# A mixture-of-experts kernel on one core: the first search candidates in one operation, one-hot rows tile by tile, w2's last quarters behind the first tokens, the last block in halves

## The chip, the core and the metric

The kernel runs on one core of a Trainium2 chip. The metric is the device time of one execution in microseconds, and the number that counts is the median of several runs. The engines of a core work beside each other and meet at semaphores: TensorE (PE) multiplies matrices, VectorE (DVE), ScalarE (ACT) and GpSimd (POOL) work on rows, SyncE (SP) issues plain transfers, and GpSimd issues the gathers and scatters by index.

## What is computed

```python
x = x + tanh(g_xattn) * wkv(time_decay, time_first, k=layernorm(x), v=ctx)   # 8 x 256 tokens, 512 channels
f = layernorm(x).reshape(2048, 512)
logits = f @ Wg + bg                       # 4 experts
top_vals, top_idx = top_k(logits, 2)
probs = softmax(logits kept at the top 2, -inf elsewhere)
out = zeros_like(f)
for i in range(4):
    score = where(expert i is in the top 2, probs[:, i], -inf)
    sel_p, sel_idx = top_k(score, 512)     # the expert takes its 512 best tokens
    p = where(isfinite(sel_p), sel_p, 0)
    h = gelu(f[sel_idx] @ W1[i])           # 512 x 2048
    out = out.at[sel_idx].add((h @ W2[i]) * p)
x = x + tanh(g_ffn) * out
```

## The kernel before, in words

**Stages.** From 0 to about 95 us the attention part runs, channel tile by channel tile (a scan on VectorE), and writes the new x to the result and its normalised rows to a table in HBM (`xn2_table`). Then comes the router, then for each expert a list of 512 tokens. The rows of the list are gathered from the table into `tok` (4 tiles of 128 tokens), transposed by TensorE, and split into a high and a low f16 half (`tok_hi` by ScalarE, `tok_lo` by VectorE). The weights are split in the same way, after a scale is taken from their magnitudes (`w1_hi`, `w1_lo`, `w2_hi`, `w2_lo`). Each product is thus three f16 products. The hidden rows are made in 16 blocks of 128, four PSUM banks at a time; for expert 0 the first four blocks are made in `first_group` (L742), token half by token half, the other twelve in `first_up` (L779), for experts 1 to 3 all in `up_product` (L801). Behind them `down_block` (L816) makes the output of 128 tokens at a time: 48 products of 512 columns (16 hidden blocks, three products each), scaled by VectorE (`take_y`, L1732) and added to the result by a scatter of GpSimd (L1213).

**The list of expert 0.** The smallest probability still taken is found digit by digit: six rounds of 5 bits (`ROUNDS0`, `DIGIT0`). Each of 128 partitions holds one candidate of 32 (`LANES0`). A round is, on VectorE: count how many probabilities reach the candidate (L1531), spread the count over the lanes (`spot`, L1540), a small step of other work (`between(r)`), then, when TensorE has added the counts over the partitions (L657), count the lanes that reach 512 (`reached`, L1543), take the digit from it (L1546), and make the next candidate from digit and `nxt` (L1549, L1552). `base` holds the digits found (L1533, L1535), `nxt` is base with the next round's lane (L1538); both stand ahead of `spot`. Then come the prefix sums, `slot_b` and `slot_a` (a token's place within a tile of the list, and the tile), `in_a`, `put` (L1646), and the one-hot rows `hot`: 16 token tiles of 128 columns, in two operations of 8 tiles (L1653). TensorE multiplies `hot` by `put`, 8 products per operation (L690), and the result is the list (`idx`, L1662).

**Order around it.** All orders are written by hand. ScalarE takes, in this order: the w1 halves, the magnitudes of w2's second quarter, a copy for the other experts' search, the copies `tok_hi` of tokens 0 and 1 (L1078), the magnitudes of w2's third quarter (L1024), the copies of tokens 2 and 3, the magnitudes of the fourth. VectorE: the lows of both token halves (L1739), the first quarter of w1_lo (L1684), `wtop` from w2's magnitudes (L1677), a step of the other experts' search, `wall` (L1462; it needs a transpose of `wtop`, which TensorE does behind the products of the second half), the scale, the second quarter of w1_lo; for this last one `first_up` waits. TensorE: two rounds for the other experts with four products between them that only keep it busy (`keep_warm`, L718), the transposes of tokens 0 and 1 (L734), the high products of the first half, the transposes of tokens 2 and 3, the low products, then the same of the second half.

**Transfers.** SyncE issues w2 of expert 0 in four quarters of 1 MB (`first_w2`, L535), the last three in a row behind the stores of x1 and of the table. GpSimd gathers once with indices that are all zero into the fourth tile of `tok` (L1228) before the list is there, and issues the fourth real gather behind its landing; then it issues the four gathers of `gather(0)` (L1204). The small constant matrices `less16`, `group16` and `tri16` are made on VectorE, within the search.

## Time and profile before

| | us |
|---|---|
| median of 3 runs | 478.41 (478.31 to 478.71) |
| the profiled execution | 478.91 |
| its span | 477.1 |
| TensorE busy | 414.5 (87%) |
| ScalarE busy | 310.1 (65%) |
| VectorE busy | 293.1 (61%) |
| GpSimd busy | 107.2 (22%) |

The profile is of one execution; times in it count from the start of its span. A row of a timeline says when an instruction started, how long it took, on which engine and line, and in brackets how long the engine had stood idle before it and what released it. Idle time of an engine matters only where others wait for it.

### The profile page before, as it was taken

To read this page: it belongs to the slowest core of one execution; us is meant where nothing else is said; L and a number is where in the kernel's file an instruction comes from. 1 tells how busy PE (TensorE), PEld (TensorE's weight loads), DVE (VectorE), ACT (ScalarE), POOL (GpSimd) and SP (SyncE) were. 2 spreads that over 40 slices of the span, in tenths; PEclk is the share of its full clock that TensorE was granted. 3 is DMA by queue.
4 is the path that set the end of the run, shared out by engine and by line. 5 is a ranking of instruction groups with operands and counts; after the bars stand their busy time and mean duration, and the time that the engine had idled before them with its cause. 6 is when DMAs were issued, how large, how long until landed. Compare 5 with 4: busy or idle time off the path is not lost.

```text
span 477.1 us, 7133 instructions
## 1 busy us (share of the span) xinstructions
PE 414.5 (87%) x2039; PEld 201.4 (42%) x2039; DVE 293.1 (61%) x600; ACT 310.1 (65%) x477; POOL 107.2 (22%) x122
## 2 busy tenths in 40 slices
PE   2586877812799999999999999999999999999991
PEld 2342433401564444454444444444444444444440
DVE  7999999988499976564675156357514635560000
ACT  6578888998569873936778790577879147770000
POOL 0777746601300002521001311100041110001111
PEclk9999998965699999999999999999999999999996
DMA  7984120399400829439001925600093310001211
GB/s 263 341 354 177 44 77 13 141 344 357 149 1 1 326 91 311 97 61 350 0 0 44 374 63 174 228 0 1 3 371 88 42 26 0 0 0 9 36 22 22
DMA packets 23126, 59.64 MB, mean 125 GB/s; under 512 B 1280, under 2 KB 1408, under 8 KB 21056
## 3 DMA queue, kind: packets, MB, share of 16 engines
q1 hardware_dynamic: 19008, 50.17, 28.4%
q0 software_dynamic: 3664, 8.65, 9.0%
q10 hardware_dynamic: 432, 0.54, 0.3%
q8 instruction: 11, 0.18, 0.1%
q14 instruction: 11, 0.09, 0.1%
HBM read 46.78 MB, written 12.58 MB: 124 GB/s over the span
## 4 chain that ended last, share of the span: by engine, by line
PE 73%; DVE 18%; issue 3%; ACT 2%; DMA 2%; POOL 0%; DVEq 0%; POOLq 0%
PE ps L816 35%; PE ps L801 26%; DVE arena L1275 7%; PE ps L779 7%; PE ps L742 2%; DVE arena L1294 2%; DVE arena L1305 2%; DVE bn L1260 1%; PE ps L712 1%; DMA arena<-xn_table,idx 1%; DVE arena L1531 1%; DMA small<-in_scalars 1%; DVE arena L1282 1%; DVE arena L1290 1%; PE ps L734 1%
## 5 line engine op out<-in xcount | busy, mean ns | idle before, releaser
L816 PE MATMUL ps<-arena 128*128 128x512 f16 x768 | 167.7, 379 | 0.0
L801 PE MATMUL ps<-arena,early 128*128 128x512 f16 x576 | 124.8, 379 | 0.0
L816 PEld LDWEIGHTS ps<-arena 128*128 128x128 f16 x768 | 74.7, 98 | 88.0
L801 PEld LDWEIGHTS ps<-arena,early 128*128 x576 | 56.4, 98 | 68.0
L1042 ACT ACTIVATE arena<-ps,up 128x512 f32<-128x512 f32 x64 | 43.8, 684 | 58.5 <-PE ps L801 40.0
L1704 DVE SCALAR_TENSOR_TENSOR arena<-arena,h_down 128x512 f32 x48 | 36.1, 751 | 58.9 <-ACT arena L1045 58.9
L1213 POOL DMA_INDIRECT result<-arena,idx x16 | 27.6, 1723 | 191.4 <-DVE arena L1732 137.8
L1045 ACT ACTIVATE arena<-arena,h_down 128x512 f32 x64 | 46.2, 721 | 8.7 <-ACT arena L1042 0.2
L1684 DVE SCALAR_TENSOR_TENSOR early<-w_raw,down,early 128x2048 f16<-128x2048 f32 x16 | 37.1, 2346 | 18.9 <-ACT early L1003 18.8
L1732 DVE TENSOR_SCALAR arena<-ps,yscale 128x512 f32<-128x512 f32 x16 | 12.0, 748 | 58.6 <-PE ps L816 49.1
L1048 ACT ACTIVATE arena<-rows,down x64 | 45.2, 706 | 0.0
L1003 ACT ACTIVATE early<-w_raw,down 128x2048 f16<-128x2048 f32 x16 | 30.7, 1990 | 14.6 <-DVE down L1479 14.6
L1204 POOL DMA_INDIRECT arena<-xn_table,idx x16 | 16.6, 1036 | 97.1 <-DVE plist L1667 93.2
L570 PE MATMUL ps<-cst,early 128*128 128x128 f32 x64 | 13.8, 329 | 27.0 <-DVE arena L1290 11.9
L1275 DVE TENSOR_TENSOR_SCAN arena<-arena,ps 128x1024 f32<-128x1024 f32 (+1 forms) x20 | 37.0, 1852 | 0.0
L1707 DVE SCALAR_TENSOR_TENSOR arena<-rows,down,arena x48 | 35.8, 746 | 0.0
L1024 ACT ACTIVATE arena<-rows 128x2048 bf16<-128x2048 f32 x16 | 30.4, 1900 | 1.7 <-DMA rows<-in_L_ffn_W 1.7
L779 PE MATMUL ps<-arena,early 128*128 128x512 f16 x144 | 31.4, 379 | 0.0
L1011 ACT ACTIVATE arena<-w_raw 128x2048 bf16<-128x2048 f32 x12 | 22.8, 1897 | 2.9 <-DVE arena L1714 1.8
L1143 POOL TENSOR_TENSOR arena<-arena 128x512 f32<-128x512 f32 (+1 forms) x19 | 20.4, 1074 | 17.9 <-ACT arena L938 17.5
L570 PEld LDWEIGHTS ps<-cst,early 128*128 128x128 f32 x64 | 8.1, 160 | 34.8 <-DVE arena L1290 17.3
L779 PEld LDWEIGHTS ps<-arena,early 128*128 128x128 f16 x144 | 13.7, 97 | 16.8 <-DVE early L1684 0.4
(226 smaller groups left out, 457.4 us busy)
## 6 DMA issues: line engine op xcount, KB each, us to landing
w_raw<-in_L_ffn_W SPq DMA_DIRECT2D x4, 4096.0 KB, 13.7
rows<-in_L_ffn_W SPq DMA_DIRECT2D x3, 4096.0 KB, 17.9
rows<-in_L_ffn_W SPq DMA_DIRECT2D x4, 1024.0 KB, 9.2
result<-rows SPq DMA_DIRECT2D x3, 1024.0 KB, 6.8
early<-in_ctx SPq DMA_DIRECT2D x2, 1024.0 KB, 6.6
rows<-in_x SPq DMA_DIRECT2D x2, 1024.0 KB, 11.8
xn_table<-arena SPq DMA_DIRECT2D x4, 512.0 KB, 5.2
xn_table<-arena SPq DMA_DIRECT2D x2, 1024.0 KB, 4.6
```

Of the source, the lines that this page charges most:

```text
L779: last = nc.tensor.matmul(ps[:, PH[q], :], w[:, k, b * P:(b + 1) * P], t[:, k, :], start=n == 0, stop=n == 3 * CT - 1)
L801: last = nc.tensor.matmul(ps[:, PH[q], :], w[:, k, at], t[:, k, :], start=n == 0, stop=n == 3 * CT - 1)
L816: last = nc.tensor.matmul(ps[:, PY[s % 2], :], h[:, t, s * P:(s + 1) * P], w[:, t, :], start=t == 0 and n == 0, stop=t == HT - 1 and n == 2)
L1003: nc.scalar.activation(w1_hi[:, k, :], w1_raw[:, k, :], ACT.Copy, scale=down[:, 0:1]).then_inc(c_w1hi, 1)
L1024: nc.scalar.activation(spent[:, k % 2, :], some, ACT.Abs, scale=1.0 / (HT * D // CT), accum_out=wmax[:, 1, k:k + 1]).then_inc(c_w2sum, 1)
L1042: nc.scalar.activation(h_f[:, q, :], ps[:, PH[q], :], ACT.Gelu, scale=up[:, 0:1]).then_inc(c_gelu, 1)
L1045: nc.scalar.activation(h_hi[:, bass.ds(at, 1), :].rearrange("p a d -> p (a d)"), h_f[:, q, :], ACT.Copy, scale=h_down[:, 0:1]).then_inc(c_ ...
L1048: nc.scalar.activation(w2_hi[:, bass.ds(at, 1), :].rearrange("p a d -> p (a d)"), w2_raw[:, bass.ds(at, 1), :].rearrange("p a d -> p (a d) ...
L1275: nc.vector.tensor_tensor_scan(state[:, u % 2, 1:size + 1], decay[:, u % CT, 0:size], pair(u, 0, size), 0.0, ALU.mult, ALU.add).then_inc(s ...
L1684: nc.vector.scalar_tensor_tensor(w1_lo[:, :, some], w1_raw[:, :, some], down[:, 0:1], w1_hi[:, :, some], ALU.mult, ALU.subtract).then_inc( ...
L1704: nc.vector.scalar_tensor_tensor(row(h_lo), h_f[:, q, :], h_down[:, 0:1], row(h_hi), ALU.mult, ALU.subtract).then_inc(c_hlo, 1)
L1707: nc.vector.scalar_tensor_tensor(row(w2_lo), row(w2_raw), down[:, 1:2], row(w2_hi), ALU.mult, ALU.subtract).then_inc(c_w2lo, 1)
```

## The change

It does the following.

- **Search.** For the first three rounds (`EXACT0` = 3) the next candidate comes in one operation from the number of lanes reached (`took`), as took x step + a prepared sum; the constant table has three more columns for it (`C_NEXT0`). The sums (`sum_next`, `sum_base`) are made by `add_steps`, behind `spot`. `base` and `nxt` stand behind `spot` in all rounds. The rounds from the fourth on keep digit and candidate apart.
- **One-hot rows.** `first_slots` makes expert 0's `hot` in 16 operations of 128 columns, from an f16 row of 0 to 127 (`iota16`) and `slot_f`, a float copy of `slot_b`; TensorE waits tile by tile.
- **Small matrices.** `less16`, `group16`, `tri16` and `iota16` are made on GpSimd, ahead of the lists.
- **Transfers.** The gather with zero indices is gone. SyncE waits for the landing of tokens 0 and 1 before it issues the third and fourth quarter of w2.
- **keep_warm.** Four more products that only keep TensorE busy stand ahead of the first tokens.
- **Last block.** The last 128 tokens of expert 3 are computed in two column halves of 256, in two PSUM banks (`last_halves`), each scaled, and scattered to a view of the result in half rows, with the indices `idx_half`.

```diff
-C_ALL = C_LANE0 + ROUNDS0
+C_NEXT0 = C_LANE0 + ROUNDS0
+EXACT0 = 3
+C_ALL = C_NEXT0 + EXACT0
...
+def ones0(r):
+
+    return sum(1 << shift0(i) for i in range(r + 1))
...
-    t[:, C_LANE0:] = np.concatenate([lane << shift0(r) for r in range(ROUNDS0)], 1).astype(np.int32).view(np.float32)
+    for r in range(EXACT0):
+        t[:, C_NEXT0 + r] = (lane[:, 0] << shift0(r + 1)) - ones0(r)
+    t[:, C_LANE0:C_NEXT0] = np.concatenate([lane << shift0(r) for r in range(ROUNDS0)], 1).astype(np.int32).view(np.float32)
...
             first_w2(1, (2,))
+            for k in range(SPT):
+                sp.wait_ge(c_tok[k], 16)
             first_w2(2, (3,))
             first_w2(3, (4,))
...
             for t in range(TT):
-                if t % (TT // 2) == 0:
-                    pe.wait_ge(b_hot, t // (TT // 2) + 1)
+                pe.wait_ge(b_hot, t + 1)
                 last = nc.tensor.matmul(ps[:, PI, 0:ST * 4], hot[:, t, :], put[:, 0, t, :], start=t == 0, stop=t == TT - 1)
             last.then_inc(b_hotused, 1)
...
                 keep_warm(WARM)
                 others_round(1)
+                keep_warm(WARM)
                 pe.wait_ge(b_taken, 2)
...
+            def last_halves():
+
+                for n in range(2):
+                    cols = slice(n * D // 2, (n + 1) * D // 2)
+                    pe.wait_ge(c_yout, START + (E - 1) * ST + (ST - 2))
+                    for t in range(HT):
+                        for i, (h, w) in enumerate(((h_hi, w2_hi), (h_hi, w2_lo), (h_lo, w2_hi))):
+                            last = nc.tensor.matmul(ps[:, LAST[n], 0:D // 2], h[:, t, (ST - 1) * P:ST * P], w[:, t, cols],
+                                                    start=t == 0 and i == 0, stop=t == HT - 1 and i == 2)
+                    last.then_inc(c_y, 1)
...
-            for s in range(ST):
+            for s in range(ST - 1):
                 down_block(E - 1, s)
+            last_halves()
...
+            pool.wait_ge(s_cst, 16)
+            nc.gpsimd.tensor_copy(iota16[:, :], cst[:, C_IOTA:C_IOTA + P]).then_inc(s_lists, 1)
+            nc.gpsimd.tensor_scalar(less16[:, :], cst[:, C_TRI:C_TRI + P], -1.0, None, ALU.add).then_inc(s_lists, 1)
+            nc.gpsimd.tensor_copy(group16[:, :], cst[:, C_GRP:C_GRP + P]).then_inc(s_lists, 1)
+            nc.gpsimd.tensor_copy(tri16[:, :], cst[:, C_TRI:C_TRI + P]).then_inc(s_lists, 1)
...
-            nc.gpsimd.memset(none[:, :], 0).then_inc(c_zero, 1)
-            pool.wait_ge(c_zero, 1)
-            nc.gpsimd.indirect_dma_start(tok[:, ST - 1, :], None, xn2_table, bass.IndirectOffsetOnAxis(ap=none[:, 0:1], axis=0),
-                                         bounds_check=N - 1, compute_op=ALU.bypass).then_inc(c_none, 16)
             gather(0)
...
-            scatter(E - 1, range(ST))
-            added(E - 1)
+            scatter(E - 1, range(ST - 1))
+            pool.wait_ge(c_yscs, START + 2 * E + 2)
+            for n in range(2):
+                cols = slice(n * D // 2, (n + 1) * D // 2)
+                pool.wait_ge(c_yout, START + (E - 1) * ST + ST + n)
+                hold(pool, "pool")
+                nc.gpsimd.indirect_dma_start(out_halves, bass.IndirectOffsetOnAxis(ap=idx_half[:, n:n + 1], axis=0),
+                                             y_c[:, (ST - 1) % 2, cols], None,
+                                             bounds_check=2 * N - 1, compute_op=ALU.add).then_inc(c_last[n], 16)
...
+            def add_steps(r):
+
+                size = float(1 << shift0(r - 1))
+                if r > 1:
+                    dve.wait_ge(b_sums, made[r - 2])
+                if r < EXACT0:
+                    for k in range(r, EXACT0):
+                        plus = cst[:, C_NEXT0 + k:C_NEXT0 + k + 1] if r == 1 else sum_next[:, k - 1:k]
+                        nc.vector.tensor_scalar(sum_next[:, k - 1:k], took[:, r - 1:r], size, plus, ALU.mult, ALU.add).then_inc(b_sums, 1)
+                    plus = -float(ones0(EXACT0 - 1)) if r == 1 else sum_base[:, r - 2:r - 1]
+                    nc.vector.tensor_scalar(sum_base[:, r - 1:r], took[:, r - 1:r], size, plus, ALU.mult, ALU.add).then_inc(b_sums, 1)
+                else:
+                    nc.vector.tensor_scalar(base[:, 0:1], took[:, r - 1:r], size, sum_base[:, r - 2:r - 1],
+                                            ALU.mult, ALU.add).then_inc(b_base, 1)
 
...
-                if r == 1:
-                    nc.vector.tensor_copy(base[:, 0:1], digit[:, 0:1]).then_inc(b_base, 1)
-                if r > 1:
-                    nc.vector.tensor_tensor(base[:, 0:1], base[:, 0:1], digit[:, 0:1], ALU.bitwise_or).then_inc(b_base, 1)
-                if 0 < r < ROUNDS0 - 1:
-                    dve.wait_ge(b_base, r)
-                    nc.vector.tensor_tensor(nxt[:, 0:1], base[:, 0:1], lane0(r + 1), ALU.bitwise_or).then_inc(b_next, 1)
                 dve.wait_ge(b_cnt, r + 1)
                 nc.vector.tensor_scalar(spot[:, :], cst[:, C_ONE0:C_ONE0 + LANES0], cnt[:, 0:1], None, ALU.mult).then_inc(b_spot, 1)
+                if 0 < r <= EXACT0:
+                    add_steps(r)
+                if r > EXACT0:
+                    nc.vector.tensor_tensor(base[:, 0:1], base[:, 0:1], digit[:, 0:1], ALU.bitwise_or).then_inc(b_base, 1)
+                if EXACT0 <= r < ROUNDS0 - 1:
+                    dve.wait_ge(b_base, r - EXACT0 + 1)
+                    nc.vector.tensor_tensor(nxt[:, 0:1], base[:, 0:1], lane0(r + 1), ALU.bitwise_or).then_inc(b_next, 1)
                 between(r)
                 dve.wait_ge(b_lane_n, r + 1)
                 nc.vector.tensor_scalar(reached[:, :], ps[:, PC, 0:LANES0], float(CAP), None, ALU.is_ge, ALU.add,
-                                        accum_out=steps_up[:, 0:1]).then_inc(b_reached, 1)
+                                        accum_out=took[:, r:r + 1]).then_inc(b_reached, 1)
                 dve.wait_ge(b_reached, r + 1)
-                nc.vector.tensor_scalar(digit[:, 0:1], steps_up[:, 0:1], -1.0, float(1 << shift0(r)), ALU.add, ALU.mult).then_inc(b_digit, 1)
-                dve.wait_ge(b_digit, r + 1)
-                if r == 0:
-                    nc.vector.tensor_tensor(cand[:, 0:1], digit[:, 0:1], lane0(1), ALU.bitwise_or).then_inc(b_cand, 1)
-                elif r < ROUNDS0 - 1:
-                    dve.wait_ge(b_next, r)
+                if r < EXACT0:
+                    if r > 0:
+                        dve.wait_ge(b_sums, summed[r - 1])
+                    plus = cst[:, C_NEXT0:C_NEXT0 + 1] if r == 0 else sum_next[:, r - 1:r]
+                    nc.vector.tensor_scalar(cand[:, 0:1], took[:, r:r + 1], float(1 << shift0(r)), plus,
+                                            ALU.mult, ALU.add).then_inc(b_cand, 1)
+                else:
+                    nc.vector.tensor_scalar(digit[:, 0:1], took[:, r:r + 1], -1.0, float(1 << shift0(r)), ALU.add, ALU.mult).then_inc(b_digit, 1)
+                    dve.wait_ge(b_digit, r - EXACT0 + 1)
+                if EXACT0 <= r < ROUNDS0 - 1:
+                    dve.wait_ge(b_next, r - EXACT0 + 1)
                     nc.vector.tensor_tensor(cand[:, 0:1], digit[:, 0:1], nxt[:, 0:1], ALU.bitwise_or).then_inc(b_cand, 1)
-            dve.wait_ge(b_base, ROUNDS0 - 1)
+            dve.wait_ge(b_base, ROUNDS0 - EXACT0)
...
-            step(nc.vector.tensor_scalar(slot_a[:, 0, :], posi[:, 0, :], 7, None, ALU.logical_shift_right), 2)
+            nc.vector.tensor_scalar(slot_a[:, 0, :], posi[:, 0, :], 7, None, ALU.logical_shift_right).then_inc(b_dve, 1)
+            steps[0] += 2
+            dve.wait_ge(b_dve, steps[0] - 1)
+            step(nc.vector.tensor_copy(slot_f[:, :], slot_b[:, 0, :]))
...
+            def first_slots():
+
+                nc.vector.tensor_tensor(put[:, 0, :, :].rearrange("p t (a c) -> p t a c", a=ST),
+                                        in_a[:, 0].unsqueeze(3).to_broadcast([P, TT, ST, 4]),
+                                        vals[:, 0].unsqueeze(2).to_broadcast([P, TT, ST, 4]), ALU.mult)
+                dve.wait_ge(s_lists, 1)
+                for t in range(TT):
+                    nc.vector.tensor_scalar(hot[:, t, :], iota16[:, :], slot_f[:, t:t + 1], None, ALU.is_equal).then_inc(b_hot, 1)
...
+                dve.wait_ge(b_taken, 2 * E)
+                nc.vector.tensor_scalar(idx_half[:, n:n + 1], idx[:, E - 1, ST - 1:ST], 1, n,
+                                        ALU.logical_shift_left, ALU.bitwise_or).then_inc(c_yscs, 1)
+            for s in range(ST - 1):
                 take_y(E - 1, s)
...
+            dve.wait_ge(c_add[1], 16 * ((E - 1) * (ST // 2) + 1))
+            for n in range(2):
+                cols = slice(n * D // 2, (n + 1) * D // 2)
+                dve.wait_ge(c_y, START + (E - 1) * ST + ST + n)
+                nc.vector.tensor_scalar(y_c[:, (ST - 1) % 2, cols], ps[:, LAST[n], 0:D // 2], yscale[:, ST - 1:ST], None,
+                                        ALU.mult).then_inc(c_yout, 1)
```

On VectorE, the third round of expert 0's search (its start is the count with `cand`) in the kernel before, and then in the changed one:

```order
L1531 TENSOR_SCALAR arena,cnt<-ps,cand 128x512
L1535 TENSOR_TENSOR base<-base,digit 128x1
L1538 TENSOR_TENSOR nxt<-base,cst 128x1
L1540 TENSOR_SCALAR spot<-cst,cnt 128x32
L1462 TENSOR_REDUCE wall<-ps 128x1
L1543 TENSOR_SCALAR reached,steps_up<-ps 128x32
L1546 TENSOR_SCALAR digit<-steps_up 128x1
L1552 TENSOR_TENSOR cand<-digit,nxt 128x1
```

Two operations stand ahead of `spot`, and two between reached and the next count. Changed:

```order
L1586 TENSOR_SCALAR arena,cnt<-ps,cand 128x512
L1588 TENSOR_SCALAR spot<-cst,cnt 128x32
L1563 TENSOR_SCALAR sum_next<-took,sum_next 128x1
L1565 TENSOR_SCALAR sum_base<-took,sum_base 128x1
L1502 TENSOR_REDUCE wall<-ps 128x1
L1598 TENSOR_SCALAR reached,took<-ps 128x32
L1605 TENSOR_SCALAR cand<-took,sum_next 128x1
```

`spot` follows its count directly, two sums stand behind it, and one operation instead of two lies between reached and the next count.

On VectorE, from the places to the list of expert 0, before and then changed:

```order
L1569 TENSOR_SCALAR slot_b<-posi 128x16
L1570 TENSOR_SCALAR slot_a<-posi 128x16
L1571 TENSOR_TENSOR in_a<-slot_a,cst 128x64
L1646 TENSOR_TENSOR put<-in_a,vals 128x256
L1653 TENSOR_TENSOR arena<-cst,slot_b 128x1024 x2
L1662 CAST idx<-ps 128x4
```

The whole of `hot` is two operations. Changed:

```order
L1629 TENSOR_SCALAR slot_b<-posi 128x16
L1630 TENSOR_SCALAR slot_a<-posi 128x16
L1633 CAST slot_f<-slot_b 128x16
L1634 TENSOR_TENSOR in_a<-slot_a,cst 128x64
L1709 TENSOR_TENSOR put<-in_a,vals 128x256
L1714 TENSOR_SCALAR arena<-iota,slot_f 128x128 x16
L1734 CAST idx<-ps 128x4
```

Sixteen operations stand for two, and the `slot_f` cast is new.

On SyncE, the transfers around w2's quarters (rows<-in_L_ffn_W) in the changed kernel, with the semaphores that each waits for:

```order
L542 DMA xn_table<-arena 128x2x512 [waits last_xn2_ready,xn2_ready]
L549 DMA rows<-in_L_ffn_W 128x4x512 [waits x1_stored_2]
L549 DMA rows<-in_L_ffn_W 128x4x512 [waits x1_stored_3,tokens_landed_1,tokens_landed_0]
L549 DMA rows<-in_L_ffn_W 128x4x512 [waits x1_stored_4]
L564 UNCONDITIONAL_BRANCH
```

Before, the third and fourth quarter waited for the stores of x1 alone.

## Rows read from the trace of the kernel before

**Rows 1.** The page's chain by line; the chain in order: start us, us, what.
```profile
PE ps L816 35%; PE ps L801 26%; DVE arena L1275 7%; PE ps L779 7%; PE ps L742 2%; DVE arena L1294 2%; DVE arena L1305 2%; DVE bn L1260 1%; PE ps L712 1%; DMA arena<-xn_table,idx 1%; DVE arena L1531 1%; DMA small<-in_scalars 1%; DVE arena L1282 1%; DVE arena L1290 1%; PE ps L734 1%
...
425.88 41.45 PE ps L816 x192
```
**Rows 2.** Stretches: us, busy PE, PEld, DVE, ACT, POOL (x), PE clock, DMA share, GB/s.
```profile
99.00:113.00 14.00, 3.62 (x15) 2.07 (x15) 12.19 (x69) 11.79 (x17) 0.00 (x0) 0.50 0.99 334
124.40:139.10 14.70, 14.36 (x98) 10.75 (x98) 8.49 (x17) 8.18 (x12) 0.45 (x2) 0.86 0.09 26
139.10:170.30 31.20, 31.20 (x149) 14.17 (x149) 30.14 (x71) 27.06 (x42) 0.00 (x0) 1.00 0.34 136
```
**Rows 3.** Timeline of VectorE, search: start us, us, engine, line, operation, tiles.
```profile
104.14 0.15 DVE L1546 TENSOR_SCALAR digit<-steps_up 128x1 int32<-128x1 f32 x1
...
104.52 0.75 DVE L1531 TENSOR_SCALAR_CACHE_REDUCE arena<-ps,cand 128x512 bf16<-128x512 f32 x1
...
105.46 0.23 DVE L1540 TENSOR_SCALAR spot<-cst,cnt 128x32 f16<-128x32 f32 x1
...
106.00 0.19 DVE L1543 TENSOR_SCALAR_CACHE_REDUCE reached<-ps 128x32 f32<-128x32 f32 x1
...
110.81 0.75 DVE L1531 TENSOR_SCALAR_CACHE_REDUCE arena<-ps,cand 128x512 bf16<-128x512 f32 x1
...
111.60 0.24 DVE L1540 TENSOR_SCALAR spot<-cst,cnt 128x32 f16<-128x32 f32 x1
```
**Rows 4.** Timeline of VectorE, small steps, one-hot rows and the list.
```profile
107.77 0.21 DVE L1507 TENSOR_SCALAR less<-cst 128x128 bf16<-128x128 f32 x1
...
112.76 0.23 DVE L1557 TENSOR_SCALAR flags<-prob,base 128x16 bf16<-128x16 f32 x1
112.91 0.23 DVE L1558 TENSOR_SCALAR flags<-prob,base 128x16 bf16<-128x16 f32 x1
...
115.37 2.35 DVE L1653 TENSOR_TENSOR arena<-cst,slot_b 128x1024 f16<-128x1024 f32 x2
118.20 0.16 DVE L1662 CAST idx<-ps 128x4 uint32<-128x4 f32 x1 [0.48 <-PE ps L690]
```
**Rows 5.** GpSimd's gathers; landing of gathers issued at 120.57 and 123.46, a store at 68.27.
```profile
114.70 1.38 POOL L1228 DMA_INDIRECT arena<-xn_table,none  x1 [0.94 <-POOL none L1226]
...
120.57 1.01 POOL L1204 DMA_INDIRECT arena<-xn_table,idx  x1 [0.30 <-issue]
...
arena<-xn_table,idx POOLq DMA_INDIRECT x1, 4.3
...
arena<-xn_table,idx POOLq DMA_INDIRECT x1, 3.5
...
result<-rows SPq DMA_DIRECT2D x1, 1024.0 KB, 4.2
```
**Rows 6.** Timeline of 126 to 136 us: ScalarE, TensorE, VectorE.
```profile
126.88 1.92 ACT L1024 ACTIVATE arena<-rows 128x2048 bf16<-128x2048 f32 x1
...
130.18 1.07 ACT L1078 CAST arena<-ps 128x512 f16<-128x512 f32 x2 [1.28 <-PE ps L734]
...
130.22 5.40 PE L742 MATMUL ps<-arena,early 128*128 128x256 f16 x48
...
134.26 0.15 DVE L1677 TENSOR_REDUCE wtop<-wmax 128x1 f32<-128x4 f32 x1
...
135.77 0.29 DVE L1462 TENSOR_REDUCE wall<-ps 128x1 f32<-128x128 f32 x1 [0.90 <-PE ps L648]
```
**Rows 7.** An idle stretch of TensorE, and the clock after it (columns as rows 2).
```profile
79.75 0.44 PE L570 MATMUL ps<-cst,early 128*128 128x128 f32 x2 [1.64 <-DVE arena L1294]
...
81.00:82.00 1.00, 1.00 (x3) 0.09 (x2) 0.93 (x3) 0.94 (x4) 1.00 (x2) 0.50 0.00 0
```
**Rows 8.** The end: the last VectorE step, the last scatter, and its landing.
```profile
467.36 0.75 DVE L1732 TENSOR_SCALAR arena<-ps,yscale 128x512 f32<-128x512 f32 x1 [9.61 <-PE ps L816]
468.98 1.55 POOL L1213 DMA_INDIRECT result<-arena,idx  x1 [8.81 <-DVE arena L1732]
...
result<-arena,idx POOLq DMA_INDIRECT x1, 4.9
```

43 lines of the change are left out of this document (25 added, 18 removed).

## The prediction

> **What bounds the kernel now.** I read the chain of waits first: of the span, 35% is the products of L816, 26% those of L801, and expert 3's 192 down products follow each other 0.216 us apart (41.45 us) [rows 1]. The table by stage narrows it. From 139.1 us on TensorE never rests (31.20 of 31.20 us busy) and has its full clock [rows 2]; the four experts come one after another. So a change can gain in two places: ahead of 139.1, by an earlier start of expert 0's second group of rows (L779), and behind the last product. The timeline of 99 to 139 us shows the first place as one string: six search rounds on VectorE, the prefix, the one-hot rows, the list at 118.20 [rows 4], the gathers [rows 5], then 14.7 us in which TensorE is nearly always busy, at a mean clock of 0.86 [rows 2].
>
> **The search.** A round ended in digit, cand, count: 104.14 to 104.52, two steps of 0.19 [rows 3]. In three rounds one step with a per-partition operand takes their place. No row has that on one column; a small step with such an operand lasts 0.23, one without 0.15 [rows 3, 4], so I take 0.26 to the next count: 0.12 saved, x 3 = 0.37. `base` and `nxt` move behind `spot`: spot comes 0.94 after its count where nxt stands ahead (104.52 to 105.46), 0.79 where it doesn't (110.81 to 111.60) [rows 3]; in four rounds 4 x 0.14 = 0.56. What moved must fit between spot and reached, 0.54 [rows 3], which TensorE's lane count sets. Steps with such an operand start 0.15 apart [rows 4]; the three or four of them in the second and third round overrun by some 0.15 in all. Together 0.78 less; bounds 0.37 (more overrun) and 1.1 (the new step at 0.19, none).
>
> **The one-hot rows.** Two operations took 2.35 us, and the list came 2.83 after their start (115.37 to 118.20) [rows 4]. Now there are sixteen of 128x128. Two neighbours with a per-partition operand start 0.15 apart though each lasts 0.23, on 16 columns; 112 more columns cost at most the 0.06 by which an f32 128x128 step (0.21) is longer than one of one column (0.15) [rows 3, 4]. Spacing 0.15 to 0.21; I take 0.17, f16 input being half as wide. 15 x 0.17, 0.25 for the last, and 0.31 from it to the list (one matmul behind it now; 0.54 from spot to reached less spot's 0.23): 3.11, which is 0.28 longer. The `slot_f` copy adds a dependent step, 0.19 less what lies beside slot_a: 0.12. **The list comes 0.78 - 0.28 - 0.12 = 0.38 earlier**; ends 1.1 earlier, 0.6 later. The Trainium skill, VectorE: DVE Perf Modes, section on the TRN2 errata, says that many small tiles pay a fixed latency per tile. Taken as no overlap at all that is a rival below.
>
> **The gathers.** The unneeded gather goes. It was also the first indirect DMA: 1.38 us on GpSimd against 1.01 for a later one [rows 5], so the first real one may now take up to 0.37 more, and the second starts that much later. w2's last two quarters no longer fill the queues: landing took 4.3 for the second gather, and 3.5 for the fourth, when they were empty [rows 5]. Second gather: 120.57 - 0.38 + 0.2 (between nothing and 0.37) + 3.5 = **123.9, against 124.9**. The second `keep_warm` stands on TensorE ahead of the tokens: four products at the half clock, 4 x 0.43, end at about 123.4, before that landing, so they cost nothing, and may bring the clock up sooner.
>
> **What is late next.** SyncE now waits for tokens 0 and 1 and issues w2's third quarter at 123.9. The nearest row, a 1 MB store into empty queues, landed after 4.2 [rows 5]; two gathers run beside it, 0.25 MB each, 0.3 to 1.6 at the 334 GB/s of [rows 2], one nearly done: I take 0.9. It lands at about 129.0 (128.3 to 130.0). ScalarE stands in order: two token copies, w2's magnitudes (which wait for that quarter), two token copies. Magnitudes to copies take 2.0, so the copies of tokens 2 and 3 start at 131.1, not 130.18 [rows 6]. Behind them wait TensorE's second half and, on VectorE, the lows, w1_low, `wtop`, a step for the other experts, and `wall`. But `wall` at 135.77 had waited 0.90 for TensorE [rows 6], so VectorE's string may come 0.9 later at no cost: 130.18 + 0.9 = 131.1. **The two just meet.** What TensorE gains ahead (about 1 us, more if its clock rises sooner) is given back in that wait; from `wall` on all is as before, and L779 starts at 139.1. Term: 0, between -0.7 and +0.9, one for one with the landing. The fourth quarter, 3 us behind at that rate (132), is needed at 131.1 + 1.07 = 132.2: nothing. The four small matrices go to GpSimd, which has no work from 99 to 113 [rows 2]: nothing; without that cover they would delay the first gather.
>
> **The end.** 48 products of 512 columns become 96 of 256: the same columns, 48 x 0.216 = 10.4 against 96 x 0.11 = 10.6 (5.40 for 48) [rows 1, 6], but the last is shorter: +0.1. The last VectorE step took 0.75 [rows 8]; at the 1.1 ns a column of the old one-hot rows 256 columns fewer save 0.28. The scatter landed 4.9 after its issue [rows 8]; half the bytes, the same 128 rows: -0.4, between 0 and -0.9. Its 1.55 on GpSimd goes by rows: 0. The first half is added 5 us earlier, beside TensorE. **-0.6**, between -0.2 and -1.2.
>
> **Sum.** 0 - 0.6 on the profiled execution: span 477.1, 478.91 with what lies around it, so 478.3. That execution is 0.5 above the median of the runs (478.41), so 477.8 to 477.9; forecast 477.9. 0.2% is 0.96 us, about what a measurement of this kernel can tell from no change.
>
> **Rivals.**
> *The quarter comes early.* It lands at 128.3 (the gathers cost it little, the one-hot rows 0.15 apart): L779 0.7 earlier, and 0.6 to 0.9 at the end: 476.9. For: landings into empty queues are short [rows 5]. Against: the gathers use the same queues. 0.27.
> *The clock falls in the new wait.* With the clock up at 125, TensorE does the first half's 40 matmuls from 125.8 at 0.11 each until 130.2, and stands until 131.8. At 78.1 to 79.75 it stood 1.64, and the clock granted soon after was 0.50 (1.2 GHz) [rows 7]. If so here, the second half's 32 products take 0.22 each until it rises, `wall` waits for TensorE, 1.5 later: 479.4, or 480 with a late quarter. It decides from an idle time of about 1.6. Against: before, the clock rose only near 128.5 (mean 0.86 over 14.7 us [rows 2]); if so again, there is hardly an idle stretch. 0.17.
> *No overlap in the one-hot rows*, the errata's rule taken fully: 16 x 0.25 = 4.0 instead of 2.35, the list 0.9 later, L779 1.2 later: 479.1. Against: the 0.15 spacing [rows 4]. 0.07.
> *The gathers are no faster*, held by GpSimd's issue and a cold first one: the edit hides nothing, the quarter lands at 129.5: 478.4. 0.06.
> *My forecast*, 477.9 (477.3 to 478.6): 0.43.
>
> **Numbers.** Faster by over 0.2% (below 477.45): the first rival and the low side of the forecast, 0.33. Slower (above 479.37): most of the clock case, half of the case without overlap, a quarter landing past 130: 0.21. Within: 0.46. The range, 476.7 to 479.5, takes in the first rival and nearly all of the clock case.
>
> **What would show it.** Count to spot 0.79 in all rounds; three rounds of 1.8 us, not 2.1; one-hot steps 0.17 apart; the list at 117.8; `wall` no longer waiting 0.90; ScalarE idle on a w2 transfer for about 2 us before its magnitudes; TensorE idle 1.5 us before the second half; L779 at 139.1; the part behind the last product 0.6 shorter. I am wrong if L779 starts outside 138.4 to 140, if TensorE's clock reads 0.5 between 130 and 136, or if ScalarE waits for something other than the third quarter.

## The result, and the profile after

| | before | after |
|---|---|---|
| median of 7 runs each, in one set | 478.71 (478.31 to 479.85) | 481.72 (480.83 to 482.95) |
| ratio of the two | | 1.0055, 95% interval 1.0043 to 1.0067 |
| the profiled execution | 478.91 | 482.27 |
| its span | 477.1 | 480.0 |

The change makes the kernel 0.55% slower. The forecast was 477.9, with the range 476.7 to 479.5; the time lies outside it, on the side to which 0.21 was given. The ratios here and below leave out two executions, 584.02 of the kernel before and 649.79 of b_warm2, that fell in a slow state.

The profiled executions stand 0.2 and 0.55 over the medians of the table, so the two spans (2.9 apart) may be read against each other. First the front. The timeline of VectorE and GpSimd in the changed kernel (start us, us, engine, line, operation, tiles; in brackets the idle time before, and its end):
```profile
100.62 0.75 DVE L1586 TENSOR_SCALAR_CACHE_REDUCE arena<-ps,cst 128x512 bf16<-128x512 f32 x1
...
102.53 0.75 DVE L1586 TENSOR_SCALAR_CACHE_REDUCE arena<-ps,cand 128x512 bf16<-128x512 f32 x1
...
104.36 0.75 DVE L1586 TENSOR_SCALAR_CACHE_REDUCE arena<-ps,cand 128x512 bf16<-128x512 f32 x1
...
106.22 0.75 DVE L1586 TENSOR_SCALAR_CACHE_REDUCE arena<-ps,cand 128x512 bf16<-128x512 f32 x1
...
114.84 2.69 DVE L1714 TENSOR_SCALAR arena<-iota,slot_f 128x128 f16<-128x128 f16 x16
117.82 0.16 DVE L1734 CAST idx<-ps 128x4 uint32<-128x4 f32 x1 [0.29 <-PE ps L706]
...
119.12 1.38 POOL L1237 DMA_INDIRECT arena<-xn_table,idx  x1 [22.25 <-DVE plist L1739]
```
The counts of the second to fourth round start 1.83 and 1.86 apart. The list comes at 117.82; it was at 118.20 [rows 4], and 117.8 was forecast. But the two searches did not start at the same time. In the kernel before the first count is this row:
```profile
100.39 0.75 DVE L1531 TENSOR_SCALAR_CACHE_REDUCE arena<-ps,cst 128x512 bf16<-128x512 f32 x1
```
From the first count to the list it was 17.81 and is 17.20, which is 0.61 less, where 0.38 was forecast; a start that came 0.23 later hides the rest. Over all the traces of this study the first count starts between 100.23 and 101.29, so a difference of a few tenths between the absolute times of two traces says little, and the distance from the first count says more. The first gather takes the 1.38 on GpSimd that the unneeded one took before [rows 5].

Then the wait. ScalarE, TensorE and one row of VectorE in the changed kernel, same view:
```profile
124.94 1.07 ACT L1107 CAST arena<-ps 128x512 f16<-128x512 f32 x2 [3.19 <-PE ps L751]
...
129.49 0.66 PE L751 MATMUL ps<-cst,arena 128*128 128x128 f32 x4 [1.48 <-DMA arena<-xn_table,idx]
...
131.97 1.91 ACT L1053 ACTIVATE arena<-rows 128x2048 bf16<-128x2048 f32 x1 [5.96 <-issue]
...
133.88 1.05 ACT L1107 CAST arena<-ps 128x512 f16<-128x512 f32 x2
...
134.50 5.33 PE L759 MATMUL ps<-arena,early 128*128 128x256 f16 x32 [2.59 <-ACT arena L1107]
...
139.99 0.29 DVE L1502 TENSOR_REDUCE wall<-ps 128x1 f32<-128x128 f32 x1 [1.43 <-PE ps L664]
```
ScalarE stands 5.96 us before the magnitudes of w2's third quarter (L1053). The copies of tokens 2 and 3 stand behind those, at 133.88 instead of 130.18 [rows 6]. TensorE stands 2.59 us for them, and its 32 products then take 5.33 us. The transfers' own rows, one by one (size, us from issue to landing), say why; the issues were at 124.22 (third quarter) and 123.44 (fourth gather):
```profile
rows<-in_L_ffn_W SPq DMA_DIRECT2D x1, 1024.0 KB, 7.7
...
arena<-xn_table,idx POOLq DMA_INDIRECT x1, 6.0
```
The quarter lands 7.7 us after its issue, at 131.9; the fourth gather takes 6.0, where it took 3.5 [rows 5]. What follows in the chain, and the clock in the stretches of it (columns as in rows 2):
```profile
124.22 0.37 SPq L549
...
124.64 9.33 DMA rows<-in_L_ffn_W
...
133.98 0.48 ACT arena L1107
...
134.50 5.33 PE ps L759 x32
...
143.40 5.31 PE ps L796 x24
```
```profile
132.00:134.50 2.50, 0.00 (x0) 0.00 (x0) 0.02 (x1) 2.50 (x4) 0.37 (x1) 1.00 0.15 56
134.50:138.50 4.00, 4.00 (x22) 2.96 (x23) 3.93 (x8) 2.34 (x3) 0.00 (x0) 0.57 0.00 0
138.50:143.40 4.90, 4.90 (x30) 2.67 (x29) 3.34 (x8) 2.32 (x4) 0.00 (x0) 1.00 0.00 0
143.40:174.60 31.20, 31.20 (x150) 14.21 (x151) 30.08 (x71) 26.98 (x42) 0.00 (x0) 1.00 0.35 136
```
The granted clock still reads 1.00 while TensorE waits (132.00 to 134.50), and 0.57 in the four us after the wait. L796 is what L779 was. It starts at 143.40 instead of 139.10, and from there the two kernels run alike: TensorE is busy for the whole of the next 31.20 us in both. The chain puts all 9.33 us on one DMA and does not show ScalarE's magnitudes between that DMA and the copies; the timeline does.

Last the end, against [rows 8]:
```profile
471.69 0.48 DVE L1902 TENSOR_SCALAR arena<-ps,yscale 128x256 f32<-128x256 f32 x1 [4.68 <-PE ps L846]
473.05 1.55 POOL L1282 DMA_INDIRECT result<-arena,idx_half  x1 [3.63 <-DVE arena L1902]
...
result<-arena,idx_half POOLq DMA_INDIRECT x1, 3.7
```
From the last VectorE step to the end of the span it is 8.3 us now and was 9.7. The balance: +4.3 at L796, -1.4 at the end, 2.9 together, which is the difference of the spans.

### The profile page after: what moved, and what is told of

It is laid out like the page before. It is cut to its first block, busy times and chain, and to the rows that moved or that the text cites. A ratio compares the mean times of both kernels' runs of the same rounds, so it can differ in the third digit from the quotient of the medians.

```text
span 480.0 us, 7258 instructions
## 1 busy us (share of the span) xinstructions
PE 419.2 (87%) x2091; PEld 207.8 (43%) x2091; DVE 293.9 (61%) x613; ACT 309.9 (65%) x477; POOL 108.7 (23%) x125
## 4 chain that ended last, share of the span: by engine, by line
PE 72%; DVE 18%; DMA 3%; issue 3%; ACT 2%; POOL 0%; DVEq 0%; SPq 0%; POOLq 0%
PE ps L833 32%; PE ps L818 26%; DVE arena L1315 7%; PE ps L796 7%; DVE arena L1334 2%; PE ps L846 2%; DMA rows<-in_L_ffn_W 2%; DVE arena L1345 2%; PE ps L759 2%; DVE bn L1300 1%; PE ps L728 1%; DVE arena L1586 1%; DMA arena<-xn_table,idx 1%; DMA small<-in_scalars 1%; PE ps L706 1%
## 5 line engine op out<-in xcount | busy, mean ns | idle before, releaser
L833 PE MATMUL ps<-arena 128*128 128x512 f16 x720 | 157.3, 379 | 0.0
L833 PEld LDWEIGHTS ps<-arena 128*128 128x128 f16 x720 | 69.9, 98 | 82.4
L1246 POOL DMA_INDIRECT result<-arena,idx x15 | 26.0, 1735 | 183.4 <-DVE arena L1804 129.0
L1053 ACT ACTIVATE arena<-rows 128x2048 bf16<-128x2048 f32 x16 | 30.4, 1899 | 8.4 <-issue 6.0
L796 PE MATMUL ps<-arena,early 128*128 128x512 f16 x144 | 31.4, 379 | 0.0
L796 PEld LDWEIGHTS ps<-arena,early 128*128 128x128 f16 x144 | 13.7, 98 | 16.7 <-DVE early L1756 0.4
```

The costliest lines, as they stand in the source:

```text
L796: last = nc.tensor.matmul(ps[:, PH[q], :], w[:, k, b * P:(b + 1) * P], t[:, k, :], start=n == 0, stop=n == 3 * CT - 1)
L833: last = nc.tensor.matmul(ps[:, PY[s % 2], :], h[:, t, s * P:(s + 1) * P], w[:, t, :], start=t == 0 and n == 0, stop=t == HT - 1 and n == 2)
L1053: nc.scalar.activation(spent[:, k % 2, :], some, ACT.Abs, scale=1.0 / (HT * D // CT), accum_out=wmax[:, 1, k:k + 1]).then_inc(c_w2sum, 1)
```

## The experiments

Theory A came from these traces: the wait that SyncE got ahead of w2's last quarters costs all of it and more, first as a late quarter (2.9 us), then as a clock that falls behind TensorE's idle time (1.4 us). Beside it stand other owners of the loss, and the parts that had been forecast one by one. Times are medians in us, with the lowest and highest in brackets; behind a ratio the brackets hold its 95% interval. The runs stand in four sets, and the kernel before ran in each; its medians were 479.16, 479.24, 479.52 and 478.98. So between sets the ratios to it are compared, and times only within a set. The ratio is not that of the medians; the two can be 0.1% apart.

### The hold undone, and the hold alone

a_nohold is the changed kernel, and b_hold the kernel before, with these two lines out and in:
```diff
             first_w2(1, (2,))
-            for k in range(SPT):
-                sp.wait_ge(c_tok[k], 16)
             first_w2(2, (3,))
```


> The changed kernel with one thing undone: SyncE no longer waits for the first two gathers before it issues w2's third and fourth quarters. Theory A (the hold costs it all: the third quarter lands 2.9 us late, TensorE idles 2.5 us and its clock falls for 1.4 us more): the quarter lands by about 121, ScalarE's copy of the third token tile is again released by TensorE near 130, L796 begins at 138.8 to 139.3 (143.40 in the changed kernel), and with the end 1.4 us shorter the time is 476.9 to 477.4, which is 1.3 to 1.8 under the kernel before and 4.3 to 4.8 under the changed one. Theory B (the search, the list or the cold gather cost part of it, the hold only the rest): L796 begins at 140.5 or later and the time is 478.5 or more. Theory C (the gathers, beside the quarters again, lose what the list gained): second gather lands at 124.9 or later, L796 at 139.5 to 140, time 477.6 to 478.1.

**Measured:** 476.47 (476.35 to 476.77), ratio 0.9940 (0.9925 to 0.9956). Without the hold the change gains 0.6% on the kernel before. The chain and a stretch of a_nohold:
```profile
125.86 1.91 PE ps L757 x16
...
128.64 5.26 PE ps L757 x48
...
134.01 3.45 PE ps L757 x16
137.47 5.31 PE ps L794 x24
```
```profile
124.40:137.40 13.00, 12.20 (x94) 9.18 (x94) 8.51 (x17) 8.21 (x12) 2.23 (x2) 1.00 0.12 36
```
Theory A is confirmed and was too small; theories B and C, with 477.6 or more, fall. L794 starts at 137.47, which is 5.9 before the changed kernel's and 1.6 before that of the kernel before. No theory had this 1.6: the list, at 117.99, is only 0.2 earlier (0.64 counted from the first count). The stretch shows where it lies: the granted clock is 1.00 (2.4 GHz) through it, where the mean was 0.86 [rows 2].

> The kernel before with one thing added: SyncE's wait for the first two gathers ahead of w2's third and fourth quarters. Theory A (the hold alone does the harm): its second gather lands 0.2 to 0.4 later than in the changed kernel, so the third quarter is issued near 124.5, lands near 132, the PE group at L742's second half waits some 2.5 us, the clock falls, and L779 begins 4 to 4.8 us later than 139.14; time 4 to 4.8 over the kernel before, 482.7 to 483.5. Theory B (the clock fall or the late quarter need the other parts of the change too, as the second keep-warm group or the tile-by-tile rows): at most 2.9 us over the kernel before, 481.6 or less.

**Measured:** 481.79 (480.78 to 483.42), ratio 1.0048 (1.0029 to 1.0067). The hold alone makes the kernel before 0.5% slower. Its profiled execution (483.42, the slowest of the six) does as theory A says: second half at 134.81 after 2.76 us of idle time, 5.33 us for its 32 products, L781 at 143.7. The median, 2.6 over the kernel before (1.4 to 3.2 by the interval), is not theory A's 4 to 4.8; it has theory B's size, at most 2.9. In the profiled execution the clock rose only at about 129 and fell again behind the wait. The other five executions left no trace, so why they are shorter is open, and theory B, that the full loss needs another part of the change too, is not excluded. On the changed kernel the hold costs more, 1.0055 against 0.9940.

### The clock kept up through the wait

a_fill, on the changed kernel, hold and all, behind each product of w1_hi and tok_lo of the first half (zero16 holds zeros):
```diff
+                    if half == 0:
+                        for i in range(24):
+                            nc.tensor.matmul(ps[:, PH[i % HB], 0:CAP // 2], zero16[:, :],
+                                             w1_hi[:, 0, 0:CAP // 2], start=False, stop=False)
```


> The changed kernel with 24 products of a zero matrix put on TensorE between the first half and the second half of expert 0's first up projection of the tokens, so that it works through most of its 2.5 us wait; they add nothing to the sums. Theory A (of the 4.26 us by which L796 is later, about 1.4 is the granted clock at half through the wait's aftermath, 2.9 the late quarter itself): the clock stays near 1.00 from 132 to 139, the x32 group takes 3.4 to 3.6 instead of 5.33, L796 begins at 141.9 to 142.4 and the time is 1.0 to 1.5 under the changed kernel, 480.2 to 480.7. Theory D (TensorE's fall costs nothing, since VectorE's string of magnitudes and powers sets L796 in any case): L796 stays at 143.2 or later and the time within 0.4 of the changed kernel.

**Measured:** 481.03 (479.97 to 482.77), ratio 1.0039 (1.0026 to 1.0052), the changed kernel's being 1.0055. Timeline and chain of a_fill:
```profile
131.96 2.78 PE L783 MATMUL ps<-early,zero 128*128 128x256 f16 x24
132.59 1.91 ACT L1058 ACTIVATE arena<-rows 128x2048 bf16<-128x2048 f32 x1 [6.31 <-issue]
...
135.12 3.67 PE L760 MATMUL ps<-arena,early 128*128 128x256 f16 x32 [0.37 <-ACT arena L1112]
```
```profile
138.79 0.30 PE ps L665
139.09 3.45 PE ps L760 x16
142.54 2.50 PE ps L801 x11
```
With 0.37 us of idle time left the clock stays up, and the 32 products take 3.67 instead of 5.33. L801 is 0.9 earlier than in the changed kernel although the quarter landed 0.6 later. From the start of the 32 products to L801 it is 7.4 us, and 8.9 in the changed kernel: the clock's fall costs 1.5 between the two traces. By the ratios it is 0.8, and their intervals overlap. Theory A's 480.2 to 480.7 was missed by 0.3, and theory D falls by its L796 of 143.2 or later. The larger part of the loss is the late quarter.

### Which quarter, and why it is slow

a_hold4 holds the fourth quarter alone; a_holdall holds both, behind all four gathers:
```diff
+            first_w2(2, (3,))
             for k in range(SPT):
                 sp.wait_ge(c_tok[k], 16)
-            first_w2(2, (3,))
```
```diff
-            for k in range(SPT):
+            for k in range(ST):
```


> The changed kernel with SyncE's wait for the first two gathers moved behind the third quarter, so that only w2's fourth quarter is held. Theory A (the third quarter's landing is what stops ScalarE and then TensorE; the fourth is asked for only by the magnitudes after the fourth token copy): the third lands by about 121, the fourth, issued near 124 and alone in the queue, by 128.5 to 131, while its magnitudes are due near 131; L796 begins at 137.4 to 138.2, and the time is 476.4 to 477.3, as with no hold at all. Theory F (the fourth quarter costs as much as the third, since the weight's power waits for it): the wait moves to the fourth quarter's magnitudes, L796 begins at 139.5 or later, and the time is 478.5 or more.

**Measured:** 476.77 (476.47 to 477.26), ratio 0.9945 (0.9932 to 0.9958). By the ratios this is the time of a_nohold; the fourth quarter can be held at no cost that they show. Its landing:
```profile
rows<-in_L_ffn_W SPq DMA_DIRECT2D x1, 1024.0 KB, 7.5
```
It lands at 132.1, later than the 128.5 to 131 expected, and ScalarE waits 1.67 for it, but with no token copy behind it. Theory F falls. The quarter was the only one in the queue here, so it is not the other quarter that makes 7.5 or 7.7 of 5.3. The fourth gather took 5.3 beside it, and L796 starts at 138.43 in this trace, 1.0 later than in a_nohold; this execution, 477.26, was the slowest of the five.

> The changed kernel with SyncE waiting for all four gathers, not the first two, ahead of w2's third and fourth quarters. Theory A1 (a 1 MB quarter issued into idle queues lands after 4.2 to 4.6 us, and the third quarter took 7.7 because it was issued among the last two gathers, the fourth gather 6.0 because of it): the fourth gather lands near 127.1, the third quarter, issued at about 127.2, lands at 131.4 to 131.9, which is no later than in the changed kernel (131.9) although it is issued 3 us later; time 481.3 to 482.2, the same as the changed kernel. Theory A2 (7.7 us is what a quarter takes there, gathers or none, as the second quarter took 8.3): it lands at 134.5 or later, L796 begins 2.5 us or more after 143.40, and the time is 484 or more.

**Measured:** 483.41 (482.80 to 484.10), ratio 1.0086 (1.0073 to 1.0099). The third quarter's landing in a_holdall, and the waits behind it:
```profile
rows<-in_L_ffn_W SPq DMA_DIRECT2D x1, 1024.0 KB, 5.3
```
```profile
127.30 0.37 SPq L549
```
```profile
132.68 1.91 ACT L1053 ACTIVATE arena<-rows 128x2048 bf16<-128x2048 f32 x1 [6.43 <-issue]
...
135.20 5.12 PE L759 MATMUL ps<-arena,early 128*128 128x256 f16 x32 [4.75 <-ACT arena L1107]
```
Issued 3.1 us later, behind the last gather's landing (127.1), the quarter lands 0.7 later, 5.3 us after its issue. So of the 7.7 some 2.4 come of the gathers beside it, and theory A2 falls. One trace shows the landing without gathers, and five show it with them: 7.5 (a_hold4), 7.7, 7.8 (a_fill), 7.9 (b_hold) and 8.1 (a_order). But 5.3 is not the 4.2 to 4.6 of A1 either. The fourth gather now took 3.6, as before the change, and not 6.0: they slow each other. The kernel is 0.3% slower than the changed one, more than the 0.5 us by which its L796 is later, and over theory A1's 482.2; TensorE's idle time of 4.75 us cost no more clock than that of 2.59 (5.12 and 5.33 for the same products).

### ScalarE's order

a_order, on the changed kernel, hold and all: the magnitudes of quarters three and four behind all four token copies.
```diff
                 nc.scalar.copy(tok_hi[half_pair(n)[1]], half_pair(n)[0]).then_inc(c_tokhi, 1)
-                if n % 2 == 1:
-                    w2_magnitudes(0, (2 + n // 2,))
+            for n in range(2):
+                w2_magnitudes(0, (2 + n,))
```


> The changed kernel, hold and all, but with ScalarE's order changed: the copies of token tiles 2 and 3 stand ahead of the magnitudes of w2's third and fourth quarters. Theory A (TensorE's wait was for a ScalarE copy that stood behind a magnitude, which waited for the late quarter): TensorE no longer idles near 132 to 134.5, its clock stays up, and L796's start is now set by VectorE's string behind the fourth quarter (landed 134.5, magnitudes 2.0, top, other experts' step, the wall), at about 139 to 142; time 478 to 481. If VectorE's string allows less than that, down to 477. Theory B (TensorE would wait anyway, for the third and fourth gathers, which landed only at 129.45): L796 stays at 143 or later and the time at 481.3 or more.

**Measured:** 480.01 (478.76 to 481.94), ratio 1.0019 (1.0003 to 1.0034). TensorE and ScalarE of a_order:
```profile
130.05 5.40 PE L759 MATMUL ps<-arena,early 128*128 128x256 f16 x48
137.61 0.32 PE L664 MATMUL ps<-cst,wtop 128*128 128x128 f32 x1 [2.16 <-DVE wtop L1749]
```
```profile
132.83 1.91 ACT L1053 ACTIVATE arena<-rows 128x2048 bf16<-128x2048 f32 x1 [1.75 <-issue]
...
135.36 1.91 ACT L1053 ACTIVATE arena<-rows 128x2048 bf16<-128x2048 f32 x1 [0.53 <-issue]
```
The second half now runs straight on from 130.05. The wait has moved to `wtop`, which needs all of w2: 2.16 us. L796 is at 141.39, 2.0 earlier than in the changed kernel and 2.3 later than before; theory A said 139 to 142, and B, 143 or later, falls. The order on ScalarE carried about a third of the hold's cost (2.0 of the 5.9 between a_nohold and the changed kernel); the quarters' landing carries the rest.

### The second keep-warm group

n_nowarm takes the second `keep_warm(WARM)` out of a_nohold; b_warm puts it into the kernel before, and nothing else:
```diff
                 others_round(1)
+                keep_warm(WARM)
                 pe.wait_ge(b_taken, 2)
```


> The changed kernel without the hold, and without its second group of four keep-warm products as well. Without the hold L794 began 1.67 us before the 139.14 of the kernel before, of which the earlier list explains 0.4. Theory W (the rest comes of the second group of keep-warm products: the granted clock rises near 124 instead of 128.6, and the transposes and the first 256-column products then take 280 and 272 ns instead of 347 and 299): the clock again rises near 128.5, the PE group before L779's successor is 1.0 to 1.4 us later, L794 begins at 138.4 to 138.9, and the time is 477.4 to 477.9, 1.0 to 1.4 over the changed kernel without the hold. Theory V (the rest comes of the gathers, which start after a list that is ready earlier and no longer behind the gather of unneeded rows; the clock gives nothing, as forecast): L794 begins within 0.4 of 137.47 and the time is 476.3 to 476.9.

**Measured:** 478.37 (476.95 to 478.94), ratio 0.9976 (0.9965 to 0.9987).

> The kernel before with one thing added: the second group of four keep-warm products between the other experts' second count and the first token tile. Theory W (the second group is what the changed front gains by, through the clock): the granted clock rises near 124 to 125 instead of 128 to 129, L779 begins at 137.5 to 138.2 (139.14 before), the time is 1.0 to 1.9 under the kernel before, and the executions lie within about 0.8 of each other instead of 2.1. Theory W2 (it needs the earlier list too, since before its four products end ahead of the tokens' landing at 124.9 and the clock falls or stays): the time is within 0.4 of the kernel before.

**Measured:** 477.34 (477.22 to 477.73), ratio 0.9964 (0.9950 to 0.9978). Two stretches each of the kernel before, of b_warm and of n_nowarm (here 2 us later), in this order:
```profile
124.00:126.00 2.00, 1.63 (x8) 1.57 (x8) 0.00 (x0) 0.08 (x1) 0.48 (x1) 0.50 0.73 193
126.00:128.00 2.00, 1.66 (x9) 1.01 (x8) 1.29 (x2) 2.00 (x3) 0.00 (x0) 0.50 0.12 47
```
```profile
124.00:126.00 2.00, 1.45 (x10) 1.13 (x10) 0.61 (x6) 0.83 (x2) 0.73 (x1) 0.90 0.70 178
126.00:128.00 2.00, 2.00 (x20) 1.83 (x19) 1.07 (x2) 2.00 (x3) 0.00 (x0) 1.00 0.24 88
```
```profile
126.00:128.00 2.00, 1.66 (x9) 1.20 (x9) 1.29 (x2) 2.00 (x3) 0.00 (x0) 0.50 0.43 125
128.00:130.00 2.00, 2.00 (x12) 1.52 (x10) 0.00 (x0) 0.64 (x2) 0.00 (x0) 0.50 0.00 0
```
Four products (1.87 us in the timeline) that compute nothing gain 2.2 us between the medians in b_warm, and 1.7 by the ratio; between a_nohold and n_nowarm the ratios differ by 1.7 us as well. In the kernel before TensorE is at the half clock (0.50, 1.2 GHz) until after 128, in b_warm it is at full from about 124.4; the 16 products of 256 columns then take 1.91 instead of 2.84. Theory W holds on both kernels, though n_nowarm is 0.5 over its 477.9 (in its trace the clock rises only after 130, and the first count starts latest of all, at 101.29). The spread says the same: 0.5 us over b_warm's seven executions, 2.4 over the 24 of the kernel before in the same set. The executions of n_nowarm fall in two heaps, four at 476.95 to 477.36 and eight at 478.07 to 478.94.

What differs ahead of the rise is 122.49 to 124.36: the four products fill it in b_warm, and in the kernel before TensorE was busy for 0.12 us of 122 to 124.

With the last block in halves (b_halves below, 0.9978) this explains a_nohold: 0.9964 x 0.9978 is 0.9942, and a_nohold has 0.9940 and 0.9942. Within the intervals nothing is left for the search, the one-hot rows and the gathers taken together.

### The search, the one-hot rows, the unneeded gather, the end

b_search is the kernel before with the changed search alone (lines as in the diff); n_oldhot is a_nohold with the rows of `slots(0)` in two operations and no `slot_f`; n_none is a_nohold with the gather of unneeded rows back; b_halves is the kernel before with the last block in halves. (b_halves, b_search and b_warm_search also lack the semaphore `c_wpow3`, for which nothing waits, and b_halves and n_none count both last scatters on one semaphore.)

> The kernel before with the changed search alone. Forecast for this part by itself: 0.78 less to the list (the profile: one-hot rows begin 0.7 to 0.9 earlier, index list near 117.4 instead of 118.20), and, with the second gather that much earlier, L779 0.5 to 0.8 earlier and the time 0.5 to 0.8 under the kernel before, 478.4 to 478.7. Theory L (what comes between the list and L779 depends on when the clock rises, by which single executions of the kernel before differ by up to 2 us, so an earlier list alone moves the median little): list as said, but the time within 0.3 of the kernel before, or even over it, as the changed kernel without hold and second group was only 0.8 under it though its end is 1.4 shorter.

**Measured:** 479.37 (478.12 to 480.17), ratio 1.0003 (0.9990 to 1.0016). The list is at 117.82, 0.38 earlier than before the change; from the first count to the list it is 17.22, 0.59 less, where 0.78 was forecast. The time is the same, and the interval excludes the 0.8 us. Theory L. A second pair ran on one chip, both with the second keep-warm group, where the clock was to be up in time in every execution:

> The kernel before with the second group of keep-warm products alone, once more, as the thing to compare the next one with on the same chip: 477.2 to 477.7, 0.3 to 0.4% under the kernel before.

> The kernel before with the second keep-warm group and the changed search. Theory X (the search alone gained nothing measurable because the time of the clock's rise, which differs from execution to execution, hid it; with the clock up in every execution the earlier list reaches L779's successor): 0.3 to 0.7 under the kernel with the second group alone. Theory Y (the path from the list to L779 has slack, since the transposes wait for keep-warm products that end after the first two gathers have landed): within 0.2 of the kernel with the second group alone.

**Measured:** b_warm2 477.70 (477.09 to 481.43), ratio 0.9981 (0.9960 to 1.0001); b_warm_search 477.55 (476.82 to 480.03), ratio 0.9980 (0.9957 to 1.0002). Theory Y by the medians, but the trace of b_warm_search (480.01) shows something else: list at 117.80, keep-warm done at about 123.4, then TensorE idle until the first gather has landed at 124.2, the clock at 0.50 until after 130, and L792 at 140.3. Here the earlier list opened a gap in front of the tokens. Five of its executions lie at 476.82 to 477.55 and four at 478.98 to 480.03. So the second keep-warm group alone does not bring the clock up early in every execution. What the search is worth with the clock surely up is not settled: the two intervals are wider than the 0.8 that was put down for it.

> The changed kernel without the hold, and with the one-hot rows made in two halves as before instead of sixteen tiles. In the traces the rows take 2.69 and the list comes 0.29 after the last of them; in two halves they took 2.35 and the list came 0.40 after. Forecast for this part: the tile-by-tile rows and their conversion cost 0.4, so undoing them brings the list from 117.8 to 117.3 to 117.6 and the time 0.2 to 0.5 under 476.47, 476.0 to 476.3. Rival (TensorE's sixteen products, which then start only behind the first half, or the clock's rise, eat the gain): the time stays at 476.4 to 476.8.

**Measured:** 475.90 (475.47 to 476.95), ratio 0.9933 (0.9916 to 0.9951). The difference from a_nohold is small, so both ran again, on one chip:

> The changed kernel without the hold and with one-hot rows in two halves, once more, on one chip with the next. If the tile-by-tile rows cost 0.4 to 0.6: 475.7 to 476.1, and 0.4 to 0.6 under the next.

> The changed kernel without the hold, once more: 476.3 to 476.7. If the 0.57 by which it stood over the kernel with one-hot rows in halves was a difference between chips, the two now lie within 0.2.

**Measured:** n_oldhot2 475.80 (475.56 to 476.19), ratio 0.9929 (0.9909 to 0.9949); a_nohold2 476.45 (476.35 to 476.70), ratio 0.9942 (0.9922 to 0.9962). VectorE of n_oldhot2, then of a_nohold2:
```profile
114.90 2.35 DVE L1723 TENSOR_TENSOR arena<-cst,slot_b 128x1024 f16<-128x1024 f32 x2
117.73 0.16 DVE L1732 CAST idx<-ps 128x4 uint32<-128x4 f32 x1 [0.47 <-PE ps L705]
```
```profile
114.97 2.68 DVE L1712 TENSOR_SCALAR arena<-iota,slot_f 128x128 f16<-128x128 f16 x16
117.94 0.16 DVE L1732 CAST idx<-ps 128x4 uint32<-128x4 f32 x1 [0.29 <-PE ps L704]
```
From the rows' start to the list it is 2.83 in halves and 2.97 by tiles; with the `slot_f` step (0.13) the tiles cost 0.27. L795 begins at 137.31 against 137.61. The time differs by 0.65, and no execution of one kernel lies within the other's; the spans differ by 0.4. (Between n_oldhot and the first a_nohold, from two sets, it is 0.3 by the ratios.) **n_oldhot is the fastest kernel of the study**, 0.7% under the kernel before and 1.2% under the changed one.

> The changed kernel without the hold, and with the gather of unneeded rows of the kernel before put back ahead of the four gathers. Theory G (the first indirect transfer is slow to start whatever it fetches, 1.38 against 1.02 us on POOL, and its rows were fetched in time that nothing waited for): the first needed gather takes 1.02 on POOL and the second is issued 0.35 us earlier, L794 begins 0.2 to 0.4 before 137.47, and the time is 476.1 to 476.3. Theory H (the gather of unneeded rows itself puts 128 rows into the queue ahead of the needed ones and waits behind w2's quarters, 8 us to its landing, so it delays what follows): the second gather lands no earlier, and the time is 476.5 or more.

**Measured:** 476.61 (476.17 to 476.89), ratio 0.9943 (0.9930 to 0.9955). The first needed gather takes 1.02 on GpSimd again (the unneeded one 1.38), and the second is issued at 120.26 instead of 120.97, yet the last of it that the trace recorded lands at 124.51, where a_nohold's came at 124.61; L796 is at 137.74 and the time that of a_nohold. The 0.7 earlier issue goes into a longer flight, beside the fourth quarter, of which the last recorded part lands at 123.2 (122.7 in a_nohold): theory H's mechanism, at a price that the times do not show.

> The kernel before with one thing added: the last block of the last expert computed, scaled and scattered in two halves. Theory A (the end is worth what the two traces show between the start of the last VectorE step and the end of the span, 9.76 against 8.33, with the products costing nothing): 1.2 to 1.5 under the kernel before, 477.2 to 477.5. As forecast (0.28 on VectorE, 0.4 on the landing, less 0.1 for the products): 0.5 to 0.7 under, 478.0 to 478.2. Theory E (the shorter landing of 3.7 to 3.8 against 4.9 in one trace is scatter between executions and not the half rows): 0.2 to 0.4 under.

**Measured:** 477.81 (476.96 to 479.37), ratio 0.9978 (0.9964 to 0.9992): 1.35 under the kernel before between the medians, and 1.05 by the ratio, whose interval (0.4 to 1.7) takes in the forecast's 0.6 and theory A's 1.4 alike. The traces decide it for theory A: from the last VectorE step to the end of the span it is 9.7 to 9.8 us in the six traces with the old end, and 8.3 to 8.5 in the twelve with the new one. The end of b_halves in its chain:
```profile
466.68 0.49 DVE arena L1854
```
It leaves 8.5 us to the end of the span (475.2), where the kernel before had 9.7; the half rows landed after 3.8.

## Why the prediction was wrong

The step that failed is the landing of w2's third quarter. It was put at 5.1 us from an issue at 123.9: 4.2, from a 1 MB store into empty queues, plus 0.9 for two gathers beside it, with bounds of 128.3 and 130.0. The runs show 7.7 (7.9 in the profiled b_hold) beside the gathers and 5.3 with none. So the nearest row was too kind by 1.1 (a store of another place, with no second transfer queued behind it), and the gathers cost 2.4 and not 0.9. The issue itself came at 124.22, 0.3 late. The quarter landed at 131.9, not 129.0.

1. **"The two just meet"** rested on that landing and fell with it. The price given, one for one with the landing, was right: 2.9 late, 2.9 of the 4.3. The path was right as well: ScalarE waited for the third quarter (5.96 us, where about 2 was said), and TensorE for the copies behind it.
2. **The clock case** was the right mechanism as a rival, at 0.17, with 1.5 us from an idle time of 1.6. The idle time was 2.59, and the fall cost 1.4 to 1.5. The fall also shows at `wall`, which waited 1.43 for TensorE where no wait was forecast. The late quarter stood beside it only as "480", although a late quarter makes that idle time: the two prices belonged in one case, 4.3 together, and the range ended at 479.5 for want of it.
3. **The second keep-warm group** was costed at nothing, with the remark that it may bring the clock up sooner and that such a gain is given back in the wait. In the changed kernel that is so: TensorE only comes to its wait sooner. But where the third quarter isn't held the clock, some 4 us sooner at full, is worth 1.7 us by the ratios in b_warm and in n_nowarm, and 0.9 in b_warm2, whose interval reaches 1.0001. The prediction gave this part no price of its own, and by the first two of these ratios it is the largest gain in the change.
4. **The search** did in the trace about what was said: spots 0.79 behind their counts, three rounds of 1.8 to 1.9. That the list came at 117.82 against a forecast 117.8 is partly luck, as the search started 0.23 later. From the first count to the rows it is 14.98 before, 14.38 in b_search and 14.08 in n_oldhot, whose front has the small matrices on GpSimd as well: 0.60 of the 0.78 came of the search alone, and another 0.30 of the matrices, for which nothing was put down. Their steps had stood between `spot` and `reached`. b_search shows no gain in time from it; the front's length hangs more on the time of the clock's rise.
5. **The one-hot rows**: 0.4 was forecast, 0.27 to 0.3 shown in the traces, and 0.3 to 0.65 in the times. The spacing is 0.163, each lasting 0.25. The rule of the Trainium skill (VectorE: DVE Perf Modes, section on the TRN2 errata) that many small tiles pay a latency each, taken as no overlap, would have made 4.0 of these 2.69; the trace does not bear that reading out. Its direction, that the large operation is the better one here, is right.
6. **The cold first gather** cost its upper bound, 0.37 where 0.2 was put in. In the changed kernel the chain runs through it: the second gather, issued 1.68 behind the first, landed at 124.17 and released the third quarter. Without the hold nobody waited for it (n_none).
7. **The end** was forecast 0.6 and is 1.4 between the traces, 1.05 by the times of b_halves. The VectorE step gave 0.27 (0.28 said). The landing gave 1.2 (4.9 to 3.7), outside its bounds of 0 and 0.9; the last products took 10.64 as said. This error went the other way and hid 0.8 us of the loss.
8. **The gathers** were to land sooner without the quarters in front of them: 3.5 us after their issue instead of 4.3. The second one took 3.4 with the hold and 3.6 without (a_nohold), where the fourth quarter was through at 122.7 by itself. So in this front the hold buys 0.2 us of flight, and the third quarter, which it moves from 120.3 to 131.9, is asked for at 126.1 (a_nohold).

## What to carry to other kernels

Before a transfer is held back, look at who waits for it in an engine's fixed order, and price it with what else will be in the queues at its new time, not with a transfer of that size alone. A late transfer and the clock that falls behind TensorE's wait for it are one case with two prices. And where the granted clock reads 0.50 in a stretch with gaps ahead of a dense one, a few products that compute nothing can be worth more than a shortening of the string beside them, as here 1.7 us against nothing that b_search shows.

## What the runs showed of the hardware

- A 1 MB load and 0.25 MB indirect gathers slow each other: the load 7.5 to 8.1 us in five traces instead of 5.3 (a_holdall), the fourth gather 5.3 to 6.0 instead of 3.5 to 3.7. In the changed kernel fifteen of the sixteen parts in which the third quarter's landing is recorded were in by 130.56 and the last came at 131.90; in a_holdall all sixteen came between 131.88 and 132.60. So there over half of the 2.4 us is one straggling part; why it straggles is not shown.
- The executions of one kernel differ by when the granted clock rises: profiled executions of two kernels with the list at 117.8 started L779's counterpart at 138.4 (b_search) and 140.3 (b_warm_search). Seven runs of kernels with the second keep-warm group and no hold on the third quarter spread by 0.4 to 1.5 us over their executions, but b_warm2 by 4.3 and b_warm_search by 3.2; kernels without it spread by 2.0 to 2.6 (1.5 in the seven executions of the first table). Single traces stand behind this, so it is a reading and not a proof.
- The granted clock read 1.00 for the whole idle time in the changed kernel, and until 0.4 us before its end in a_holdall, and 0.50 behind it. After 2.59 and after 4.75 us of idle time TensorE lost nearly the same: 32 products of 256 columns took 5.33 and 5.12 us, and 3.67 with 0.37 us of idle time.
- An indirect scatter of 128 half rows (1 KB each) landed after 3.7 to 3.8 us, of full rows (2 KB) after 4.9.
- The first indirect transfer took 1.38 us on GpSimd in every kernel, whatever it fetched, and the gathers behind it 1.01 to 1.02.
